# Patch planes written out in DRAM: both stacks of patches as one transfer each, and no copies on chip

## The reference

```python
# block 1: binary 3x3 convolution, 64 -> 64 channels
x = x + conv3x3(sign(_gn(x)), sign(weight)) * scale
# block 2: involution, 7x7 taps, 16 groups of 4 channels
v = _gn(x)
r = relu(batchnorm(w_r @ v + b_reduce))          # 16 channels
ker = (w_s @ r + b_span).reshape(B, 16, 49, H, W)  # 49 taps for every pixel and group
out[b, g, d, h, w] = sum over ki, kj of
    pad(v)[b, g, d, h + ki, w + kj] * ker[b, g, 7 * ki + kj, h, w]
x = x + out
```

## Time and profile before

| | us |
|---|---|
| median of 3 runs | 1971.62 (1965.9 to 1975.86) |
| profiled execution, its own time | 1978.51 |
| its span on the core | 1976.6 |
| TensorE matmul busy | 1621.0 (82%) |
| VectorE busy | 1378.6 (70%) |
| ScalarE busy | 1052.8 (53%), of it 736.8 in the copies (L432) |
| GpSimd busy | 1015.0 (51%) |

### The profile page before, as it was taken

The page is one execution under the profiler, slowest core; times in us unless marked ns, Lnnn a source line. Parts: engine busy times, 40 slices in busy tenths (PEclk is TensorE's granted clock), DMA queues, the critical chain, the costliest instruction groups (busy, mean ns, idle before and its releaser), DMA issues.

```text
span 1976.6 us, 39046 instructions
## 1 busy us (share of the span) xinstructions
PE 1621.0 (82%) x15072; PEld 730.2 (37%) x15072; DVE 1378.6 (70%) x1699; ACT 1052.8 (53%) x758; POOL 1015.0 (51%) x904
## 2 busy tenths in 40 slices
PE   3488897978889797896978878798887988889885
PEld 1233443434333343343433334333333433334332
DVE  5476776858768685776867767586776767768674
ACT  2255555545655554555545655465555545655562
POOL 1145555554645555455554645555455554645673
PEclk8799998999999998998989989898989999989997
DMA  4679899797998969899798998979799797998993
GB/s 106 158 168 237 185 238 224 199 233 172 245 216 217 236 173 239 186 244 215 188 240 181 250 215 205 230 183 247 175 240 225 187 250 180 248 215 205 227 243 85
DMA packets 215178, 410.70 MB, mean 208 GB/s; under 512 B 87406, under 2 KB 134815, under 8 KB 210847
## 3 DMA queue, kind: packets, MB, share of 16 engines
q1 hardware_dynamic: 139728, 356.81, 74.2%
q10 hardware_dynamic: 75264, 51.39, 10.1%
HBM read 310.30 MB, written 84.93 MB: 200 GB/s over the span
## 4 chain that ended last, share of the span: by engine, by line
POOL 46%; issue 42%; SPq 4%; DMA 2%; DVE 2%; PE 2%; ACT 1%; POOLq 1%; ACTq 0%; DVEq 0%
POOL folded L365 46%; SPq L305 2%; DMA patches<-parts_dram 1%; SPq L287 1%; PE ybank L571 1%; DMA back<-consts_dram 1%; POOLq L364 0%; SPq L257 0%; ACT patches L432 0%; DVE prod L792 0%; SPq L295 0%; PE ybank L541 0%; DMA parts_dram<-parts 0%; DVE parts L783 0%; SPq L270 0%
## 5 line engine op out<-in xcount | busy, mean ns | idle before, releaser
L365 POOL TENSOR_TENSOR folded<-prod 128x448 f32<-128x448 f32 x896 | 1009.3, 1139 | 941.3 <-DVE prod L792 940.0
L792 DVE TENSOR_TENSOR prod<-ybank,relu 128x896 f32<-128x896 f32 x896 | 961.1, 1088 | 406.9 <-PE ybank L571 333.4
L571 PE MATMUL ybank<-patches,wspan 128*64 128x448 f16 x7168 | 863.7, 382 | 240.2 <-DMA patches<-parts_dram 110.4
L432 ACT ACTIVATE patches<-patches 96x1792 f16<-96x1792 f16 x448 | 736.8, 1689 | 589.8 <-DMA patches<-parts_dram 306.9
L571 PEld LDWEIGHTS ybank<-patches,wspan 128*64 128x64 f16 x7168 | 396.3, 116 | 757.6 <-issue 416.1
L512 PE MATMUL ybank<-sgn,convw 128*128 128x448 bf16 x1008 | 205.6, 357 | 24.5 <-ACT sgn L385 20.1
L589 PE MATMUL obank<-folded,esum 128*32 128x448 f32 x1792 | 214.8, 551 | 1.5 <-POOL folded L365 1.5
L582 PE MATMUL obank<-patches,wbias 128*32 128x448 f16 x3584 | 197.8, 364 | 0.0
L512 PEld LDWEIGHTS ybank<-sgn,convw 128*128 128x128 bf16 x1008 | 93.4, 97 | 137.8 <-issue 33.5
L582 PEld LDWEIGHTS obank<-patches,wbias 128*32 128x32 f16 x3584 | 87.4, 99 | 105.2 <-issue 52.7
L783 DVE TENSOR_TENSOR parts<-ybank,parts 128x1024 f16<-128x1024 f32 x64 | 78.5, 1226 | 60.5 <-ACT parts L404 60.5
(11 more groups left out here) (90 smaller groups left out, 380.0 us busy)
## 6 DMA issues: line engine op xcount, KB each, us to landing
patches<-parts_dram SPq DMA_DIRECT2D x1120, 224.0 KB, 7.0
parts_dram<-parts SPq DMA_DIRECT2D x128, 256.0 KB, 7.7
xs<-x_dram SPq DMA_DIRECT2D x128, 196.0 KB, 5.0
sums_dram<-osb ACTq DMA_DIRECT2D x112, 224.0 KB, 6.2
rows<-sums_dram ACTq DMA_DIRECT2D x112, 224.0 KB, 6.6
out_dram<-xs SPq DMA_DIRECT2D x128, 196.0 KB, 3.7
relu<-blocks SPq DMA_DIRECT2D x256, 49.0 KB
patches<-gb_dram SPq DMA_DIRECT2D x1, 784.0 KB
```

Source lines behind the costliest of these rows:

```text
L365: pool.tensor_tensor(folded[:, u % 8, :], prod[:, u % 2, 0, :], prod[:, u % 2, 1, :], ALU.add).then_inc(fold_done, 1)
L432: act.activation(X2[0:COPIED_ROWS, e % 2, at], X1[0:COPIED_ROWS, e % 3, at], ACT.Copy).then_inc(copied, 1)
L571: mm = pe.matmul(bank("unit", p, n)[64 * t:64 * t + 64, h, 0:N], wspan[:, stack, g, h, :], of_group(e, stack, g), start=(stack == 0), stop ...
L792: dve.tensor_tensor(prod[:, u % 2].rearrange("m h (n c) -> m h n c", c=GC), bank("unit", p, n)[:, :, 0:N].rearrange("m h (n c) -> m h n c" ...
```

## The change

Planes are laid out in DRAM in the form in which a stack reads them. `D0` and `D1`, one for each stack tile, have for each pair buffer 128 rows of `Q = 8` planes of `RUN = 2048` fp16. `parts_out` writes each part several times: once into every plane that holds it, shifted by the plane's rows. Row 8r + q of a stack tile is then partition row r of plane q, and a stack is one DMA of 128 partitions x 4 runs of 3584 B. `X2` is loaded whole (its seventh plane has zero weights and is filled with finite values); `copy_high`, its semaphore and its waits are gone. The selection matrix is permuted to the new row order. `load` and `store` become one DMA of 128 partitions each.

```diff
-PLANES = (((0, 0, 32, 4), (0, 4, 0, 2), (0, 1, 33, 4), (1, 0, 96, 2),
-           (0, 2, 34, 4), (1, 1, 1, 2), (0, 3, 35, 4), (1, 2, 97, 2)),
-          ((0, 0, 32, 4), (0, 4, 0, 2), (0, 1, 33, 4), (0, 2, 34, 4), (0, 3, 35, 4),
-           (1, 3, 96, 2), (1, 4, 97, 2)))
+PLANES = (((0, 0), (0, 2), (0, 4), (1, 1), (0, 1), (0, 3), (1, 0), (1, 2)),
+          ((0, 0), (0, 2), (0, 4), (1, 3), (0, 1), (0, 3), None, (1, 4)))
+Q = 8
+RUN, BLOCK = 2048, 128
-FIRSTLOAD, SECONDLOAD = 16 * 8, 16 * 2
-DWRITE = 16 * 2
+FIRSTLOAD, SECONDLOAD = 16, 16
+DWRITE = (16 * 16, 16 * 9)
-        D = nc.dram_tensor("parts_dram", (2, 2, 128, PART), F16, kind="Internal").ap()
+        D0 = nc.dram_tensor("planes_dram", (2, 128, Q, RUN), F16, kind="Internal").ap()
+        D1 = nc.dram_tensor("planes2_dram", (2, 128, Q, RUN), F16, kind="Internal").ap()
             def load(p):
-                for rows in ROWS16:
-                    sp.dma_start(xs[rows, p % 3, :], xv[p][rows]).then_inc(x_loaded, 16)
+                sp.dma_start(xs[:, p % 3, :], xv[p]).then_inc(x_loaded, 16)
             def parts_out(p, k):
                 sp.wait_ge(low_done, 4 * p + k + 1)
                 if p > 0:
-                    sp.wait_ge(d_written[k], DWRITE * p)
-                for l in range(2):
-                    sp.dma_start(D[p % 2, l].rearrange("m (y h n) -> m y h n", y=2, h=4)[:, :, k, :],
-                                 Ev[:, l, k % 2]).then_inc(d_written[k], 16)
+                    sp.wait_ge(d_written[k], DWRITE[k > 0] * p)
+                b = p % 2
+                def run(dram, planes, q, l, y, shift, many):
+                    src = Ev[:, l, k % 2, y]
+                    if k == 0:
+                        for i in range(many):
+                            cut = BLOCK * (shift + i)
+                            sp.dma_start(dram[b, :, q + i, 0:4 * BLOCK - cut], src[:, cut:]).then_inc(d_written[k], 16)
+                        return
+                    dst = bass.AP(tensor=dram.tensor, offset=(128 * b * planes + q) * RUN + BLOCK * (4 * k - shift),
+                                  ap=[[planes * RUN, 128], [RUN - BLOCK, many], [1, 4 * BLOCK]])
+                    sp.dma_start(dst, src.unsqueeze(1).broadcast_to((128, many, 4 * BLOCK))).then_inc(d_written[k], 16)
+                run(D0, Q, 0, 0, 0, 0, 3)
+                run(D0, Q, 4, 0, 1, 0, 2)
+                run(D0, Q, 6, 1, 0, 0, 2)
+                run(D0, Q, 3, 1, 1, 0, 1)
+                run(D1, Q, 0, 0, 0, 0, 3)
+                run(D1, Q, 4, 0, 1, 0, 2)
+                run(D1, Q, 3, 1, 1, 1, 1)
+                run(D1, Q, 6, 1, 0, 0, 1)
+                run(D1, Q, 7, 1, 0, 2, 1)
+            def stack(dram, e):
                 p = e // E
+                return bass.AP(tensor=dram.tensor, offset=(128 * (p % 2) + 4 * JX * (e % E)) * Q * RUN,
+                               ap=[[RUN, 128], [4 * Q * RUN, JX], [1, JY * 128]])
...
-                for l, a, row, step in PLANES[0]:
-                    sp.dma_start(X1[row:row + 15 * step + 1:step, e % 3, :],
-                                 plane(e, l, a)).then_inc(first_in[e % 3], 16)
+                sp.dma_start(X1[:, e % 3, :].rearrange("p (j n) -> p j n", j=JX), stack(D0, e)).then_inc(first_in[e % 3], 16)
...
-                for l, a, row, step in PLANES[1][COPIED_PLANES:]:
-                    sp.dma_start(X2[row:row + 15 * step + 1:step, e % 2, :],
-                                 plane(e, l, a)).then_inc(second_in[e % 2], 16)
+                sp.dma_start(X2[:, e % 2, :].rearrange("p (j n) -> p j n", j=JX), stack(D1, e)).then_inc(second_in[e % 2], 16)
-            def copy_high(e, j):
...
-                    pe.wait_ge(copied, JX * (e + 1))
```

More of the change, by code:

```diff
@@ L23 @@
 TAPS = K * K
-ROWS16 = tuple(slice(*r) for i in range(2) for r in ((32 + 2 * i, 96, 4), (i, 32, 2), (33 + 2 * i, 96, 4), (96 + i, 128, 2)))
 PY, PX = 4, 2
@@ L29 @@
 IY, IX = PY + K - 1, PX + K - 1
-PLANES = (((0, 0, 32, 4), (0, 4, 0, 2), (0, 1, 33, 4), (1, 0, 96, 2),
[3 rows of a table removed]
-COPIED_ROWS, COPIED_PLANES = 96, 5
+PLANES = (((0, 0), (0, 2), (0, 4), (1, 1), (0, 1), (0, 3), (1, 0), (1, 2)),
+          ((0, 0), (0, 2), (0, 4), (1, 3), (0, 1), (0, 3), None, (1, 4)))
+Q = 8
 JY, JX = H // PY, 4
@@ L67 @@
 FIRST_LOADS, LOADS, ZEROS = 16 * 2, 16 * 6, 4
-XLOAD, STORE = 16 * 8, 16 * 8
-FIRSTLOAD, SECONDLOAD = 16 * 8, 16 * 2
-COPY = JY * 128
-DWRITE = 16 * 2
+XLOAD, STORE = 16, 16
+FIRSTLOAD, SECONDLOAD = 16, 16
+DWRITE = (16 * 16, 16 * 9)
 SPREAD = 16 * 16
@@ L84 @@
 SUMS_B, BIAS, SUMS_A, ROWS_AT = 3, 6, 7, 7
-COPY_AT = {0: 0, 1: 1, 4: 2, 5: 3}
 def turns(pairs):
@@ L188, in build @@
         second_in = [sem("second_in0"), sem("second_in1")]
-        copied = sem("copied")
         r_ready = sem("r_ready")
@@ L255, in load @@
             def load(p):
-                for rows in ROWS16:
-                    sp.dma_start(xs[rows, p % 3, :], xv[p][rows]).then_inc(x_loaded, 16)
+                sp.dma_start(xs[:, p % 3, :], xv[p]).then_inc(x_loaded, 16)
             def store(p):
                 sp.wait_ge(out_added, 4 * (p + 1))
-                for rows in ROWS16:
-                    sp.dma_start(ov[p][rows], xs[rows, p % 3, :]).then_inc(stored, 16)
+                sp.dma_start(ov[p], xs[:, p % 3, :]).then_inc(stored, 16)
             def parts_out(p, k):
@@ L267, in parts_out @@
                 if p > 0:
-                    sp.wait_ge(d_written[k], DWRITE * p)
-                for l in range(2):
-                    sp.dma_start(D[p % 2, l].rearrange("m (y h n) -> m y h n", y=2, h=4)[:, :, k, :],
-                                 Ev[:, l, k % 2]).then_inc(d_written[k], 16)
-            def plane(e, l, a):
+                    sp.wait_ge(d_written[k], DWRITE[k > 0] * p)
[20 more added lines that the diff above has]
+            def stack(dram, e):
                 p = e // E
-                first = ((p % 2) * 2 + l) * 128 * PART + 4 * JX * (e % E) * PART
-                return bass.AP(tensor=D.tensor, offset=first + (a % 2) * (CY // 2) * 128 + (a // 2) * 128,
-                               ap=[[PART, 16], [4 * PART, JX], [1, JY * 128]])
+                return bass.AP(tensor=dram.tensor, offset=(128 * (p % 2) + 4 * JX * (e % E)) * Q * RUN,
+                               ap=[[RUN, 128], [4 * Q * RUN, JX], [1, JY * 128]])
             def first_stack(e):
@@ L284, in first_stack @@
                 for k in range(4):
-                    sp.wait_ge(d_written[k], DWRITE * (e // E + 1))
-                for l, a, row, step in PLANES[0]:
-                    sp.dma_start(X1[row:row + 15 * step + 1:step, e % 3, :],
-                                 plane(e, l, a)).then_inc(first_in[e % 3], 16)
+                    sp.wait_ge(d_written[k], DWRITE[k > 0] * (e // E + 1))
+                sp.dma_start(X1[:, e % 3, :].rearrange("p (j n) -> p j n", j=JX), stack(D0, e)).then_inc(first_in[e % 3], 16)
             def second_stack(e):
@@ L402, in high @@
                     before = 4 * p + k - 2
-                    act.wait_ge(d_written[before % 4], DWRITE * (before // 4 + 1))
+                    act.wait_ge(d_written[before % 4], DWRITE[before % 4 > 0] * (before // 4 + 1))
                 act.activation(Ev[:, 0, k % 2], bank("t", p, k)[:], ACT.Copy).then_inc(high_done, 1)
@@ L466, in _ @@
                 relu(0, k)
-            for j in range(JX):
-                copy_high(0, j)
             for p in range(pairs):
@@ L479, in _ @@
                         gather(e - 1)
-                    if n % GP in COPY_AT and e + 1 < EALL:
-                        copy_high(e + 1, COPY_AT[n % GP])
                     if n % GP == ROWS_AT and e > 0:
@@ L854, in constants @@
             for stack in range(2):
-                for part, a, row, step in PLANES[stack]:
+                for q, plane in enumerate(PLANES[stack]):
+                    if plane is None:
+                        continue
+                    part, a = plane
                     sel = stack if part or stack == 0 else 2
@@ L860, in constants @@
                         if 0 <= ky < K and 0 <= kx < K:
-                            c[ky * K + kx, C_SEL + 384 * pos + 128 * sel + row + step * r] = 1
+                            c[ky * K + kx, C_SEL + 384 * pos + 128 * sel + Q * r + q] = 1
     for m in range(128):
```

## The result

The changed kernel takes 2231.36 us (median of 4 runs, 2230.07 to 2232.46) against 1970.28 us before: 1.132 times as long, 95% interval 1.129 to 1.135. That is +261 us where the forecast had +106: the direction and the place are as predicted, the size is not. The profiled execution has a span of 2229.9 us, 253 more than before.

What follows compares the result with a forecast made beforehand. The seam s3 to s6 bounds the kernel, by SP's order and the DMA engines together. 1978.5 + 98 (15 seams at +6.5) + 10 (start) - 2 (end) = 2084.5, less 6.9 for the runs' median: 2078 us; range 1975 to 2320.

Steps and rivals of the forecast that it cites:

- the seam: From stack s3 to the start of s6 in each pair of images: 60.4 us, not 49.52, +10.9 us a pair.
- the mixture: Part writes and image loads together on SP's queue: 371 GB/s, taken for the whole seam's 20.95 MB.
- The waits on copies: PE's waits for ACT's patch copies, 3.10 us before s0 and 1.24 before s1, go: -4.3 us a pair.
- `high`'s new waits: high(2) and high(3) wait for plane writes, delaying s5's start by some 5 us, hidden under the seam.
- The start: Before the first stack all parts must be in DRAM, so the spread ends later: +10 us.
- The end: The last store is 1 issue, not 8: -2 us; the last pair, without planes to write, may win up to 8.
- SP alone gives almost the same: In the seam, SP's own issues would have s6's data there at 1033, against 1034.0 by the queue's bytes.
- A: Stack loads stay at 250 GB/s, bound on the DRAM side: about 2460 us; chance 0.17 with rates 250 to 320.
- B: Plane writes slow down at 32 KB steps, 250 GB/s instead of 334: +8 us a pair, 2198 us; chance 0.12.
- C: Queue reads and writes overlap throughout at 434 GB/s: 1956 us, deciding from 420; chance 0.16 including up to forecast's edge.
- D: 128-partition loads reach only the parameters' rate, 339 GB/s everywhere: 2158 us; chance 0.55 together with the forecast.
- The forecast's own condition: The forecast falls if the seam's queue moves over 420 or under 320 GB/s.

Runs made afterwards that it cites:

- e6: Changed kernel with r passed through DRAM: ACT writes it once, SP reads it back in 8 transfers behind s6's load; 2145.76 us, 1.090.
- e10: Changed kernel without the writes of the second stack's five high planes from the third pair on; 2106.60 us, 1.069.
- e2: Changed kernel with both stacks reading one set of ten planes, each stack in 4 transfers of 128 partitions; 2321.12 us, 1.176.
- e3: Changed kernel with e2's shared planes, spread issued by ACT and the image load moved from s3 to s5; 2251.32 us, 1.145.
- e8: Kernel before with r passed through DRAM, and image load and store as one DMA of 128 partitions each; 1905.47 us, 0.968.
- e9: As e8, with the ACT copy that refills r's blocks waiting for r's write only, not all its reads; 1935.52 us, 0.981.
- e12: As e9, with s0's load issued ahead of r's reads; 1922.37 us, 0.974.

## Why the direction was right and the size wrong

**Right.** The bound: the seam, and PE's wait before s6 in it. The bytes (659 MB for 655). The rates: writes alone 325 (forecast over 320), stack loads 357, the mixture 370 where the forecast took 371. The waits on copies went (-3.9 us before s0 and s1, forecast -4.3). s6 came out at 14.07 (14.2), s0 at 12.96 (12.8). `high`'s new waits delay s4 by 5.9 us (forecast 5) and are hidden: PE still waits 22.3 us in the mean before s6. The start cost 8.6 (10). The end gave 12, not 2: the last pair has no planes to write, which I had left out with "up to 8". No stage shows a gain from ACT's 720 us beyond those waits.

**The step that failed** is "SP alone gives almost the same". I worked out that SP's own chain would end at 1033 and the queue's data at 1034, and took the later, as if both ran side by side from end to end. They don't. SP did not run ahead of the full queue: it stood in the plane writes for as long as the queue needed, 25.04 us for the 18 issues that I had at 11.5, and began `spread` only then; and while it gave 16 small issues, the queue had little left to move. s6's load left 61.6 us after s3 began, not 51.9. So for each stretch the slower of the two counts, and the stretches add up. In the shown seam, against the forecast's 60.4 us from s3 to s6:

| | us |
|---|---|
| `spread`: 11.48 for 1.18 MB, which take 3.2 at 371 GB/s | +8.3 |
| the other 19.8 MB in 56.6 us, 349 GB/s, not 371 | +3.3 |
| the first load leaves 0.8 before s3, not 1.9 behind it | -2.7 |
| measured: 69.3 | +8.9 |

(1.18 MB is 11.5 us at 103 GB/s; the 56.6 us leave out the 2 that the forecast gave to the landing.) e6 shows the first line: without that stretch s5 loses 7.6 us. The second is the tail behind 1028 and the loads and writes ahead of 990, where the queue gives less than the 371 of its mixture. Of the whole +17.2 a pair, e6 accounts for 5.7. The rest is bytes and issues ahead of s6's load: e10 shows that 2.49 of the 8.0 MB of planes, with their issues, cost 8.9.

By the means, the forecast's pair of 125.1 us is 10.5 short of 135.6. The seam is 8.4 of that, and s2 is 1.6: I took s2's 16.8 from the one pair shown, where the mean before was 18.3. That pair's seam was longer than the mean by as much (49.52 for 47.94), but I built the seam anew from bytes, and so the two no longer made up for each other.

The trace of before gave a hint: in its own `spread` the share was already 0.83, below the 0.99 of s3. A faster queue could be expected to have still less left to move there.

**The rivals.** A (loads stay at 250) is refuted by the 357. B (plane writes slow at a pitch of 32 KB) is refuted by the 325 GB/s of the writes, against 334 at 8 KB; its 2198 is near the result for another reason. C asked for 420 GB/s in the seam; it was 304. D's 339 is a little under the 352 that the queue moved from 965.75 to 1016.5, and its 2158 lacks the same series. The forecast's own condition, a seam under 320 GB/s, came true.

**Left open.** How much the queue takes before it holds SP back; whether e10's 8.9 us are bytes or issues; what of the four-transfer form slows e2 and e3; what in e8's one-transfer images saves the 34 us; why e9 and e12 don't beat e8. e6 and e10 together were not run: if they add, 2231 - 86 - 125 = 2020 us, an estimate, which is still slower than before.

## What to carry to other kernels

When one engine issues everything for one queue, go through the order stretch by stretch: each costs the longer of its issuing and its data, and the stretches add up; the larger of two totals is only a lower bound. A transfer of all 128 partitions is worth having (357 GB/s for 250 in the stack loads; e8, 34 us from two small edits), but a layout that bought it with 70% more bytes in the stretch that already bounded the kernel lost. Put small issues behind the load that an engine waits for, not ahead of it, and look at once at what then waits for them.

## What the hardware showed that was not expected

The rate of a load with the same 3584 B runs went from 130 GB/s (16 neighbouring partitions per transfer) over 250 (16 partitions a step of 2 or 4 apart, from another layout in DRAM) to 357 (128 in one), each time with a share of 0.97 or more. A full queue held back the engine that issues for it: an issue of line L275 took 775 ns in the median and up to 7273. And issues on two engines' queues at once took longer than in turn: 18.94 us for ACT's 16 and 28.54 for SP's 18, against 11.48 and 25.04.
